# Attention of a decoder layer: context energy by a ones matmul, layernorm scalars per tile, two key buffers, transposes at the end of a slot

## The reference, cut to what matters

```python
x = layernorm(x + autocorrelation_attention(x))        # x: (16, 256, 2048)
x = layernorm(x + cross_attention(ctx, ctx, x))        # sim = ctx . x^T / 16, softmax over ctx rows, times ctx
x = layernorm(x + ffn(x))                              # x @ W_base.T + top-2 mixture of 8 rank-8 LoRA experts
```

## Time and profile before

| what | value |
|---|---|
| median of 3 runs | 2191.81 us (2190.49 to 2195.47) |
| the profiled execution's own time | 2195.65 us |
| its span, first to last instruction | 2193.8 us |
| mean granted TensorE clock, share of full | 0.971 |
| PE busy | 1990.9 us (91% of the span) |
| DVE busy | 988.7 us (45%) |
| ACT busy | 511.9 us (23%) |
| POOL busy | 296.7 us (14%) |
| moved by DMA | 271.13 MB, mean 124 GB/s |

### The profile page before, as it was taken

How to read it: one execution, slowest core, us unless ns; L and a number is a source line. 1 busy time by engine, 2 the same in 40 slices (tenths; PEclk the granted TensorE clock), 3 DMA queues, 4 the chain that set the end, 5 groups by cost and what they waited for, 6 DMA issues and landing times.

```text
span 2193.8 us, 27988 instructions
## 1 busy us (share of the span) xinstructions
PE 1990.9 (91%) x11232; PEld 1056.9 (48%) x11232; DVE 988.7 (45%) x2182; ACT 511.9 (23%) x691; POOL 296.7 (14%) x418
## 2 busy tenths in 40 slices
PE   1878878878888699999999999999999999999998
PEld 1655645555555344444444444444444444444443
DVE  3788878888887652232223222232223222232222
ACT  4445444544442540010001000010001000110000
POOL 1242243243242320000000000000000000000000
PEclk9999999998999799999999999999999999999999
DMA  7588678778866752232223322232223322232220
GB/s 250 135 220 256 215 205 241 245 198 233 251 184 191 256 158 58 59 105 65 57 57 91 81 58 57 65 103 62 57 57 96 76 57 57 71 100 59 57 58 39
DMA packets 288907, 271.13 MB, mean 124 GB/s; under 512 B 261504, under 2 KB 261632, under 8 KB 265984
## 3 DMA queue, kind: packets, MB, share of 16 engines
q1 hardware_dynamic: 288832, 270.17, 42.4%
HBM read 138.02 MB, written 67.11 MB: 94 GB/s over the span
## 4 chain that ended last, share of the span: by engine, by line
PE 64%; ACT 1%; DMA 1%; POOL 1%; DVE 0%; issue 0%; ACTq 0%; SPq 0%; POOLq 0%
PE ps_y_f L1097 59%; PE ps_a_f L1116 1%; PE ps_y_f L1101 1%; PE ps_y_f L1102 1%; DMA chunk<-w_chunks 1%; PE ps_a_f L1117 1%; ACT w_hi_f L892 1%; POOL w_lo_f L875 0%; POOL chunk L874 0%; DVE w_lo_f L966 0%; PE ps_h_f L1124 0%; PE ps_t_f L1082 0%; DVE b_stack_f L1052 0%; ACT y_f L953 0%; ACT b_stack_f L950 0%
## 5 line engine op out<-in xcount | busy, mean ns | idle before, releaser
L1097 PE MATMUL ps_y_f<-w_hi_f,x_hi_f 128*128 128x512 f16 x2048 | 777.8, 380 | 9.9 <-POOL w_lo_f L875 7.4
L1097 PE MATMUL ps_y_f<-w_hi_f,x_lo_f 128*128 128x512 f16 x2048 | 778.0, 380 | 0.0
L1097 PE MATMUL ps_y_f<-w_lo_f,x_hi_f 128*128 128x512 f16 x2048 | 777.9, 380 | 0.0
L953 ACT ACTIVATE y_f<-y_f,nb_f,rs_f 128x2048 f32<-128x2048 f32 x32 | 67.0, 2093 | 1112.4 <-POOL nb_f L883 1112.4
L1097 PEld LDWEIGHTS ps_y_f<-w_hi_f,x_hi_f 128*128 128x128 f16 x2048 | 200.7, 98 | 246.8 <-POOL w_lo_f L875 9.6
L1097 PEld LDWEIGHTS ps_y_f<-w_hi_f,x_lo_f 128*128 128x128 f16 x2048 | 200.8, 98 | 242.6 <-issue 1.6
L1097 PEld LDWEIGHTS ps_y_f<-w_lo_f,x_hi_f 128*128 128x128 f16 x2048 | 200.7, 98 | 233.9 <-issue 1.4
L977 DVE SCALAR_TENSOR_TENSOR y_f<-ps_y_f,w_iscale,xn_f 128x512 f32<-128x512 f32 x64 | 46.6, 749 | 476.9 <-PE ps_y_f L1102 476.9
L977 DVE SCALAR_TENSOR_TENSOR y_f<-ps_y_f,w_iscale,xn 128x512 f32<-128x512 f32 x64 | 46.6, 748 | 447.9 <-PE ps_y_f L1102 447.9
L610 PE MATMUL ps_t_fast<-ident,xbuf_fast 128*128 128x128 f32 x512 | 95.5, 334 | 134.1 <-ACT xbuf_fast L413 116.3
L880 POOL TENSOR_TENSOR var_eps_f<-mv_f,columns 128x1 f32<-128x1 f32 x32 | 6.1, 191 | 1356.9 <-DVE mv_f L1065 1356.9
(11 more groups left out here) (146 smaller groups left out, 2055.2 us busy)
## 6 DMA issues: line engine op xcount, KB each, us to landing
cbuf_fast<-ctx_in SPq DMA_DIRECT2D x32, 1024.0 KB, 6.1
xbuf_fast<-x SPq DMA_DIRECT2D x32, 1024.0 KB, 8.8
x_scratch<-x2buf_fast SPq DMA_DIRECT2D x32, 1024.0 KB, 11.7
out<-y_f SPq DMA_DIRECT2D x32, 1024.0 KB, 4.1
xn<-w_chunks SPq DMA_DIRECT2D x16, 1024.0 KB, 8.4
xn<-x_scratch SPq DMA_DIRECT2D x16, 1024.0 KB, 4.8
xn_f<-x_scratch SPq DMA_DIRECT2D x16, 1024.0 KB, 4.8
chunk<-w_chunks SPq DMA_DIRECT2D x18, 512.0 KB, 5.6
```

The lines of the kernel that those rows point to most:

```text
L953: nc.scalar.activation(y[parity][:], y[parity][:], ACT.Identity, bias=nb_[:, 0:1], scale=rs[:, 0:1]).then_inc(out_ready, 1)
L1097: nc.tensor.matmul(ps_y[j][:], xx[parity][:, k], ww[:, k, j * BANK:(j + 1) * BANK], start=(k == 0 and xx is x_hi and ww is w_hi), stop=False)
```

## The change

- The sum over partitions of the context's squares is a matmul with a 128x128 tile of ones, float32, 4 columns, on PE behind context(6) and the last transposes (`context_energy`); it writes to free columns of the PSUM bank of logits(1). POOL's reduce is gone from the slots. DVE computes the scales before the last statistics of batch n.
- The layernorm scalars of x are computed for each tile by itself on POOL, in the order fold(0), norm of batch n, norm(0), fold(1), norm(1). ACT normalises both tiles: tile 0 behind exp(0), tile 1 behind exp(1). The two squares of weights stand between them, and in place, with no tile for their output. DVE's normalisation of tile 1 is gone.
- There are two buffers for keys. SP's order in a slot is now store, weights, x, and then the transposes of batch n+2 and the context loads of batch n+3.
- Memory: context tile 0 lies where two prefetched weight chunks of the feed-forward go, the transposed fold where `ag_raw` goes, so the prefetches wait also for the last forward transform and the last v_lo. An unused float16 identity goes.

```diff
+        u_t = consts["ag_raw"][:, 0:HALF // P * C // 2].bitcast(BF16).rearrange("p (k c) -> p k c", c=C)
...
+        sumall = ps_s[1][:, C:C + PIECES]
...
                         if (part, r) == (0, 0):
-                            after(sp, sim_done, R * n)
+                            after(sp, sim_done, R * (n - 1))
                         sp.wait_ge((vhi_done, vlo_done)[part], R * n + r + 1)
-                        sp.dma_start_transpose(k_both[:, :, part, r * P:(r + 1) * P],
+                        sp.dma_start_transpose(k_both[parity][:, :, part, r * P:(r + 1) * P],
                                                (v_hi, v_lo)[part][parity][:, r]).then_inc(k_turned, 16)
...
-                        transpose_keys(n + 1, 1 - parity, 0, 0)
-                        transpose_keys(n + 1, 1 - parity, 0, 1)
-                        for r in range(R):
-                            transpose_keys(n + 1, 1 - parity, 1, r)
-                            load_context(n + 2, r)
+                        store(n - 1, 1 - parity)
                         load_weights(n + 2)
-                        store(n - 1, 1 - parity)
                         load_x(n + 2, parity)
+                    for r in range(R):
+                        transpose_keys(n + 2, parity, 0, r)
+                    for r in range(R):
+                        transpose_keys(n + 2, parity, 1, r)
+                        load_context(n + 3, r)
...
+                sp.wait_ge(fwd_done, 4 * nb)
+                sp.wait_ge(vlo_done, R * nb)
...
                     def fold(r):
                         if n2:
+                            if r == 0:
+                                after(pool, t_filled, TB * (n + 1) + ORDER.index("u1") + 1)
                             pool.wait_ge(x_loaded[parity][r], 16 * (half + 2))
                             g.tensor_tensor(u_rows[:, r], xbuf[parity][:, r, 0:HALF], xbuf[parity][:, r, HALF:L],
                                             ALU.subtract).then_inc(folded, 1)
-                    def reduce_context():
+                    def norm1(r):
                         if n2:
-                            pool.wait_ge(sumsq_done, PIECES * (n + 3))
-                            settle(0)
-                            g.partition_all_reduce(sumall[parity][:], sumsq[parity][:], P,
-                                                   bass.bass_isa.ReduceOp.add).then_inc(sumall_done, 1)
-                    reduce_context()
-                    if n2:
-                        after(pool, t_filled, TB * (n + 1) + ORDER.index("u1") + 1)
+                            pool.wait_ge(mv1_ready, R * (n + 2) + r + 1)
+                            after(pool, x1_ready[r], n + 2)
+                            norm_steps(0, mv1, eps_column, slice(r, r + 1), rs1, nb1, ln1_ready)
                     fold(0)
                     if cur:
                         pool.wait_ge(mv2_ready, n + 1)
                         after(pool, x2_ready, R * n)
-                        norm_steps(1, mv2, EPS_AT, rs2[:], nb2[:], ln2_ready)
+                        norm_steps(1, mv2, EPS_AT, slice(0, R), rs2, nb2, ln2_ready)
+                    norm1(0)
                     fold(1)
+                    norm1(1)
                     if n2:
-                        pool.wait_ge(mv1_ready, n + 3)
-                        for r in range(R):
-                            after(pool, x1_ready[r], n + 2)
-                        g.tensor_tensor(mean_sq[:], mv1[:, :, 0], mv1[:, :, 0], ALU.mult)
-                        norm_steps(0, mv1, eps_column, rs1[:], nb1[:], ln1_ready)
-                        pool.wait_ge(ln1_ready, n + 3)
+                        chain.link(g.tensor_tensor(mean_sq[:], mv1[:, :, 0], mv1[:, :, 0], ALU.mult))
                         g.tensor_tensor(g_energy[:, bass.ds((n + 2) * R, R)], mean_sq[:], mv1[:, :, 1], ALU.add).then_inc(mv1_free, 1)
...
-                    def normalise1():
+                    def normalise1(r):
                         if n2:
-                            act.wait_ge(ln1_ready, n + 3)
-                            act.wait_ge(folded, R * (n + 2) + 1)
-                            nc.scalar.activation(xbuf[parity][:, 0], xbuf[parity][:, 0], ACT.Identity, bias=nb1[:, 0:1],
-                                                 scale=rs1[:, 0:1]).then_inc(x1_ready[0], 1)
+                            act.wait_ge(ln1_ready, R * (n + 2) + r + 1)
+                            act.wait_ge(folded, R * (n + 2) + r + 1)
+                            nc.scalar.activation(xbuf[parity][:, r], xbuf[parity][:, r], ACT.Identity, bias=nb1[:, r:r + 1],
+                                                 scale=rs1[:, r:r + 1]).then_inc(x1_ready[r], 1)
...
                             square_context(j - 1)
-                        if j >= 6 and not (isinstance(n, int) and n == -2):
-                            square_weights(j - 6)
...
                     softmax_exp(0)
-                    if isinstance(n, int) and n == -2:
-                        square_weights(0)
-                        square_weights(1)
-                    normalise1()
+                    normalise1(0)
+                    square_weights(0)
+                    square_weights(1)
                     softmax_exp(1)
+                    normalise1(1)
...
+                    if n2:
+                        dve.wait_ge(sumall_done, n + 3)
+                        chain.link(v.tensor_reduce(tmp[:, 0:1], sumall, AX.X, ALU.add))
+                        scale_steps(nc, chain, scale[parity][:], iscale[parity][:], tmp[:, 0:1], tmp2[:, 0:1])
+                        v.tensor_scalar(lscale[parity][:], iscale[parity][:], C ** -0.5, None, ALU.mult).then_inc(scale_ready, 1)
...
-                                chain.link(ins)
-                            else:
-                                ins.then_inc(mv1_ready, 1)
-                    if n2:
-                        dve.wait_ge(sumall_done, n + 3)
-                        chain.link(v.tensor_reduce(tmp[:, 0:1], sumall[parity][:], AX.X, ALU.add))
-                        scale_steps(nc, chain, scale[parity][:], iscale[parity][:], tmp[:, 0:1], tmp2[:, 0:1])
-                        v.tensor_scalar(lscale[parity][:], iscale[parity][:], C ** -0.5, None, ALU.mult).then_inc(scale_ready, 1)
+                            ins.then_inc(mv1_ready, 1)
                     x_stats(0)
                     value_low(0)
                     softmax_max(0)
@@ -570,12 +560,6 @@
                     value_low(1)
                     softmax_max(1)
                     softmax_norm(1)
-                    if n2:
-                        dve.wait_ge(ln1_ready, n + 3)
-                        dve.wait_ge(folded, R * (n + 2) + 2)
-                        v.tensor_scalar(xbuf[parity][:, 1], xbuf[parity][:, 1], rs1[:, 1:2], nb1[:, 1:2], ALU.mult,
-                                        ALU.add).then_inc(x1_ready[1], 1)
...
+                    def context_energy():
+                        if n2:
+                            pe.wait_ge(sumsq_done, PIECES * (n + 3))
+                            if n == -2:
+                                pe.wait_ge(w_cleared, 2)
+                            after(pe, scale_ready, n + 2)
+                            nc.tensor.matmul(sumall, ones[:], sumsq[parity][:], start=True, stop=True).then_inc(sumall_done, 1)
...
+                        if j == 6:
+                            context_energy()
...
+        halves = consts["cbuf0"][:].rearrange("p (h k c) -> p h k c", h=2, k=KC)
+        consts["chunks"] = [halves[:, 0], halves[:, 1], consts["chunk2"][:]]
```

48 lines of the change are left out of this document (22 added, 26 removed).

## The result

The change took the kernel from 2191.99 to 2132.15 us (medians of four runs each, all runs between 2190.49 and 2195.47, and 2131.03 and 2133.39): ratio 0.9725, 95% interval 0.9708 to 0.9742. That is 59.8 us faster, where I had forecast 94, and 1.2 us above the upper end of my range. The profiled execution took 2132.35 us with a span of 2130.4 us, 63.4 us less than the span of 2193.8 us before.

The account below looks back on a forecast made before the run. POOL's late scalars, delayed by its sum over partitions, were taken to hold the attention slots. Start 26.8 + 13 x (41.79 - 36.4) - tail 3.7 = 93.2 us gained, giving 2098 us, range 2076 to 2131.

Parts of the forecast that it names:

- one instruction is waited for, not the queue behind it: DVE and POOL meeting: DVE waits only for POOL's current instruction and comes in ahead of POOL's next one.
- the term of 0.4 us for POOL's scaling beside p_hi(1): End of the slot on DVE: p_hi(1) meets the first half of POOL's x2 scaling, adding 0.4 us to the period.
- The waits say what holds it: Attention slots before: ACT's tile 0 normalisation waits for POOL's last scalar, 144.7 us; PE waits for that normalisation, 116.3 us.
- SP, transposes and loads ... free: SP's queue: v_hi transposes no longer wait for logits(1) and run while DMA is idle, at no cost.
- The new period, 36.4 us: Attention slot, set by DVE's chain to p_ready: 36.4 us against 41.79, bounds 35.3 and 38.4.
- The second case: Rival: POOL and DVE hold each other longer, p_hi(1) behind both scaling halves; period 38.4, 2126 us; chance 0.22.
- near 1: PE's granted clock in the attention slots, 0.93 on average before, should rise to near 1.
- The start, 26.8 us: Before slot 1: its T0 comes at 95.8 instead of 122.62, 26.8 us earlier.
- The tail, +3.7: Weights' sum at the end, now first of its kind: 9.51 instead of 5.76 us, costing 3.7, bounds 0 and 3.7.
- The transfers: Rival: DMA binds, transposes holding back x tiles or context tile 1 by 3 us; period 39.4, 2140 us; chance 0.12.
- fold(0) does wait for x: Rival: POOL's fold(0) waits for x, not the sum; period 39 at best, or unchanged at 2190 us; chance 0.05.
- No x tile came late behind a transpose: Rival, slower: v_hi transposes served ahead of x tile 1; its landing at T0+34 gives 2209 us; chance 0.05.

Follow-up runs that it names:

- the second half held back: The changed kernel, with POOL waiting for p_ready of batch n+1 before the second half of its x2 scaling: 2089.83 us, ratio 0.9515.
- PE filled: The changed kernel with 14 matmuls that compute nothing added before context(0) of each slot, where PE waited for p_lo: 2116.88 us, ratio 0.9642.
- the two experiments on it: On the kernel with POOL's second scaling half waiting: guard tables loaded behind first transposes and context tiles, 2087.8 us; plus slot -1's context squares behind all evacuations, 2085.94 us.
- the versions of 35.2 us: The changed kernel with all of POOL's scaling behind p_lo (2090.86 us, period 35.17), or only the second half (2089.83 us, period 35.22).

## Why the prediction was wrong

The forecast counted a gain of 93.2 us of the span; it was 63.4. The step that failed is "one instruction is waited for, not the queue behind it", and with it the term of 0.4 us for POOL's scaling beside p_hi(1), which measured 2.1: in 13 slots and slot 14 that is some 23 of the 29.8 us that are missing. The start is most of the rest. The steps in their order:

- **"The waits say what holds it"** (ACT for POOL's last scalar): wrong as a statement of what bounds the kernel before. I had ranked the engines' waits and left out the queue of SP, whose waits the same view shows; these rows stand in it for the kernel before:

```profile
ACT junk_fast L391 <- DMA cbuf_fast<-ctx_in: 79.1, 29, 6.5
...
SPq L245 <- PE ps_s_fast L639: 113.7, 15, 9.8
```

  The loop through keys, context tiles and squares held 41.6 to 41.8 us a slot by itself (41.82 and 41.62 with POOL's sum out of it), POOL's chain 39.1. POOL's scalars were late in part because its sum was fed late: the squares released its spacer at T0+11.0 (466.85) in the kernel before and at T0+8.5 (470.47 less 461.93) with the second key buffer.
- **"SP, transposes and loads ... free"**: I counted the second key buffer at no cost, which held, and gave it no gain, which was the largest error of attribution: with SP's order it brings 40 us. My sum contained its gain unnamed, because I took the period from DVE's chain with nothing else in the way, and there the loop was gone. That the sum didn't suffer was luck; a reader who had built the ones matmul first, for the reason that I gave, would have seen 0.3%.
- **The new period, 36.4 us.** That p_lo, behind v_lo(1), would be late next was right. From v_lo(1) to the next T0 I had 2.7 + 2.1 + 0.4 = 5.2 us; it is 6.96 (439.74 to 446.70), and 5.30 with the second half held back. What failed is the term "p_hi(1) meets its first half: 0.4". The meeting with p_hi is there (0.81 for 0.39), and then p_lo meets the second half. **"So one instruction is waited for, not the queue behind it"** is true of one instruction of DVE, but DVE has two in a row, 0.04 us apart, and POOL's next one comes ahead of the second. The term is 0.42 + 1.67 = 2.1 us instead of 0.4. The trace of the kernel before shows this too, in slot 6, where p_hi(0) ended at 361.26 and fold(1) began ahead of p_lo(0), which then took 2.60 us; my working leaves it out:

```profile
361.27 2.34 POOL L323 TENSOR_TENSOR u_rows_fast<-xbuf_fast 128x1024 bf16<-128x1024 f32 x1
361.30 2.60 DVE L540 SCALAR_TENSOR_TENSOR p_lo_fast<-expd_fast,rinv_fast,p_hi_fast 128x256 f16<-128x256 f32 x1
```

  From T0 to v_lo(1) I had 31.2 us, 30.5 and 0.7 for fold(1) meeting p_hi(0). The changed kernel takes the same 31.2 (38.18 - 6.96), but by luck: that meeting did not come (p_hi(0) takes 0.39), the stretch is 29.9 us long where the clock is 1.00 (35.22 - 5.30), and the clock, the next point, put 1.3 us back. The second case had the price of the whole, 38.4 against 38.18 measured, by another way (p_hi behind both halves). The rule of the Trainium skill that I had weighed (SBUF — State Buffer, "SBUF: two separate sides": whoever starts first holds the port pair for its whole instruction) fits in kind all three meetings: p_hi and p_lo that wait for POOL, and POOL's 3.08 us behind DVE's 1.34. By it alone I had worked out 38.0. The Trainium skill ties the lock there to instructions of DVE in a 2-port mode or with two inputs in SBUF; p_lo has two such inputs, and no run here tests the condition.
- **The clock.** I had "near 1". An idle stretch of 3.5 us before context(0) in each slot kept its mean at 0.95; filling it brought 1.00 and 1.30 us a slot. So p_lo's lateness counts 1.67 and costs 2.96. In the forecast this term was 0, as the idle stretch was 1 to 2 us in it; with 1.9 us of idle (the second half held back) the clock is indeed 1.00. Period in all: 38.18 - 36.4 = 1.8, which is p_lo's 1.67, with the clock's 1.3 against the 1.3 that I had too much; 23.3 us over 13 slots, and 2.0 in slot 14. Slot 14 is 32.14 us long with the second half held back and 34.1 with PE filled, so that is p_lo's wait too.
- **The start, 26.8 us**: 20.2. Of the 6.6 us missing, 5.1 lie ahead of T0 of slot 0 (64.46 for 59.4), and 1.6 are slot 0's own length (37.98 for 36.4). The first transposes came at 23.05 (forecast 23.5), so sum, statistics and scalars were right. But the two v_hi transposes took 7.62 us to issue behind the loads of the tables, the context tiles of batch 1 went out at 27.67 and 34.02, and ACT's squares held its evacuations up. My text has no term for the transposes there; the two experiments on it gave back 2.9 and another 1.2 us.
- **The tail, +3.7**: 0. The weights' sum, now the first of its kind, took what it took before, and the Trainium skill's figure for a first call (about 6 us; GPSIMD Engine Reference, 2.1 Instruction dispatch) agrees in size:

```profile
653.31 0.40 POOL L357 PARTITION_ALL_REDUCE w_total_all_fast<-w_total_fast  x1 [5.62 <-issue]
```

  But the rows do not tie it to the first call: in the kernel before, each of the 16 sums behind the first stood behind 5.76 to 7.27 us too, the 5.76 us of the earlier trace rows, which I had taken for agreement with the rule, among them. And the 9.51 us of the earlier trace rows are no price of being the first alone; the three other kernels with a sum at that place have 8.63, 8.85 and 9.35 there. What makes it longer at the start was not tried. Behind this row the rest took 1477.1 us instead of 1475.3; that 1.8 us was not followed up.

The parts against the forecast: start -6.6, slots -23.3, slot 14 -2.0, tail +3.9, feed-forward -1.8, together 29.8 us missing. Of the rivals, POOL and DVE holding each other was the one that came (0.22 in my chances), though not as written: p_hi did not wait for both halves, and my sign of it, p_hi over 2 us, did not show (0.81); the 2.15 us are p_lo's. The transfers did not bind: DMA is busy 0.93 in the versions of 35.2 us. fold(0) does wait for x, at no cost. No x tile came late behind a transpose.

One thing stays open in part. Sum on POOL with scalars by tile (40.07) and scalars together with the ones matmul (40.29) are both longer than sum on POOL with scalars together (39.27); the first two have slots of about 39.5 and of about 40.8 us. The granted clock goes with the length in the second of them (0.94 in one of 39.63, 0.92 in two of 40.8), but not in the first (0.96 and 0.93 in two short slots, 0.92 and 0.94 in two long ones). Their rows show other meetings of DVE and POOL. With the sum on POOL and scalars by tile, p_lo(1) takes 2.15 us in slots 2 to 13, with scalars together 0.48; and in three long slots of the first kernel exp(1) starts at T0+36.5, 6.7 us behind the start of v_lo(1): in slot 7 the last scalar of tile 0 comes just behind v_lo(1) and takes 2.34 us (384.85), and ACT's normalisation, which stands ahead of exp(1), waits for it. With scalars together and the ones matmul, v_lo(0) takes 3.38 us or more in slots 2 to 13, against 2.28 in the changed kernel. I have no run that moves one of these meetings alone, so that they make the difference is not shown.

## What to carry to other kernels

Before ranking waits, look for loops that go from one slot to the next, and read the queues that issue transfers beside the engines: a part that removes the loudest wait brings nothing (0.3% here) while a second loop is as long, and the parts' values don't add (40 us for one of them, 60 for all, about 105 with one wait more).

Where POOL works beside short dependent steps of DVE, cost each step as if POOL's whole next instruction could come before it, and put a long POOL instruction behind the last of them: one semaphore wait gave 42 us here. A gap on PE costs more than its length where the clock falls in it.

## What the runs showed of the hardware that I had not expected

- POOL can begin its next instruction in a gap of 0.04 us between two instructions of DVE (361.27, between 361.26 and 361.30); a step of 0.48 us then takes 2.60, and 2.15 in the changed kernel.
- 14 matmuls for nothing in a gap of 3.5 us made the kernel 15 us faster; the granted clock went from 0.95 to 1.00. The idle stretch had put the first 4 us behind it at a mean of 0.59.
- The issue of two transposes on SP took 4.56 us at the start, or 7.43 when table loads stood ahead of them.
- A sum over partitions between other instructions of POOL costs it some 6.3 us ahead and 7.2 us behind (the kernel with the second key buffer alone), in each slot, around 0.44 us of work. Of the changed kernel's sums, the weights' cost 5.62 ahead; the guard's, the next instruction behind it, waited 1.49, and that for DVE.
